# Drains between VectorE's scans and products, and the last batch's chain inside the last group of tiles, in a graph and expert layer

## The reference, cut to what matters

```
h = (xn @ W_gat).reshape(M, 4, 4)
e = leaky_relu(a_src[src] + a_dst[dst])
ee = exp(e - segment_max(e, dst)[dst])
alpha = ee / (segment_sum(ee, dst)[dst] + 1e-16)
agg = segment_sum(h[src] * alpha[:, :, None], dst) + b_gat
scores = layernorm(agg, gamma, beta).reshape(M, 4, 4).mean(1)
w = softmax(top 2 of scores)
out = x + sum over experts e of g_e * (gelu(xn @ W1[e] + b1[e]) @ W2[e] + b2[e])
```

## Time and profile before

| what | value |
|---|---|
| median of 3 runs | 4078.52 us (4076.69 to 4079.31) |
| the profiled execution | 4079.9 us, its span 4078.1 us |
| TensorE matmuls busy | 3314.7 us (81%) |
| GpSimd busy | 2933.2 us (72%) |
| VectorE busy | 2002.3 us (49%) |
| ScalarE busy | 856.3 us (21%) |
| mean granted clock of TensorE | 0.924 of full speed |

### The profile page before, as it was taken

One profiled execution on the slowest core, in us unless ns is written; L12 is line 12 of the kernel. 1 busy time (PEld: TensorE's weight loads), 2 busy tenths in 40 slices (PEclk: granted clock), 3 DMA queues, 4 the chain that ended last, 5 costly groups with the idle time before them and its releaser, 6 DMA issues. The chain is left out here.

```text
span 4078.1 us, 46844 instructions
## 1 busy us (share of the span) xinstructions
PE 3314.7 (81%) x13237; PEld 2233.8 (55%) x13238; DVE 2002.3 (49%) x4747; ACT 856.3 (21%) x2123; POOL 2933.2 (72%) x3018
## 2 busy tenths in 40 slices
PE   0598888998886887878878699999999999994333
PEld 0355555665554655555555366666666666662222
DVE  6577776777765866665454312212223122232555
ACT  6122222222210111111111112222222222220221
POOL 2677777777777777777777777777777777774726
PEclk6799999999998999999999899999999999997665
DMA  8655554554554666667666322222222222224568
GB/s 257 180 136 135 135 135 132 136 133 133 134 140 125 173 173 169 180 174 194 178 175 176 80 79 69 62 63 70 70 70 65 65 71 62 70 73 133 155 183 257
DMA packets 379496, 530.13 MB, mean 130 GB/s; under 512 B 120955, under 2 KB 298459, under 8 KB 379224
## 3 DMA queue, kind: packets, MB, share of 16 engines
q0 software_dynamic: 122976, 244.93, 26.6%
q1 hardware_dynamic: 231599, 261.90, 20.3%
q10 hardware_dynamic: 24776, 21.73, 1.7%
HBM read 381.54 MB, written 146.74 MB: 130 GB/s over the span
## 5 line engine op out<-in xcount | busy, mean ns | idle before, releaser
L824 POOL DMA_INDIRECT rows<-xn_rows,gsrc x1664 | 1613.9, 970 | 509.8 <-issue 509.5
L1414 POOL DMA_INDIRECT nb<-route_rows,idx x1024 | 1011.5, 988 | 318.2 <-issue 303.5
L1130 PE MATMUL PS<-rows,oh 128*128 128x257 f32 x3328 | 867.3, 409 | 276.3 <-DMA rows<-xn_rows,gsrc 275.3
L1130 PEld LDWEIGHTS PS<-rows,oh 128*128 128x128 f32 x3328 | 640.8, 201 | 422.1 <-DMA rows<-xn_rows,gsrc 312.3
L1851 PE MATMUL PS<-arena,hid 128*125 128x256 f32 x3200 | 697.2, 380 | 20.9 <-ACT hid L1763 20.9
L1843 PE MATMUL PS<-x2g,arena 128*128 128x500 f32 x1600 | 676.9, 584 | 17.1 <-DMA x2g<-x_turned 17.1
L1851 PEld LDWEIGHTS PS<-arena,hid 128*125 128x125 f32 x3200 | 598.6, 188 | 129.6 <-issue 33.1
L1731 DVE TENSOR_TENSOR y_sb<-PS,b_b 125x512 f32<-125x512 f32 x200 | 128.7, 685 | 1069.6 <-PE PS L1851 1069.2
L1843 PEld LDWEIGHTS PS<-x2g,arena 128*128 128x128 f32 x1600 | 304.7, 191 | 374.9 <-issue 356.4
L1763 ACT ACTIVATE hid<-PS,b_sb 128x500 f32<-128x500 f32 x400 | 270.8, 677 | 646.5 <-PE PS L1843 646.5
L866 DVE TENSOR_TENSOR oh<-PS,rel 128x1024 f32<-128x1024 f32 x208 | 253.9, 1221 | 9.2 <-issue 1.0
(11 more groups left out here) (341 smaller groups left out, 3524.2 us busy)
## 6 DMA issues: line engine op xcount, KB each, us to landing
y_rows<-y_sb SPq DMA_DIRECT2D x100, 512.0 KB, 2.7
rows<-xn_rows,gsrc POOLq DMA_INDIRECT x1664
arena<-y_rows SPq DMA_DIRECT2D x40, 512.0 KB, 7.0
nb<-route_rows,idx POOLq DMA_INDIRECT x1024
sum_rows<-kept SPq DMA_DIRECT2D x104, 128.5 KB
x_rows<-x SPq DMA_DIRECT2D x100, 128.0 KB, 4.8
m_in<-sum_rows SPq DMA_DIRECT2D x100, 125.5 KB
x_n<-xn_rows SPq DMA_DIRECT2D x100, 125.0 KB
```

Of the source, the lines that this page charges most:

```text
L824: pool.indirect_dma_start(out=rows[w][h][:, q, 0:D], out_offset=None, in_=xn_rows, in_offset=bass.IndirectOffsetOnAxis(ap=gsrc[:, s * HU + ...
L1130: last = mm(SUM[:, 0:D + 1], oh[w][h][:, q, :], rows[w][h][:, q, :], start=h == 0 and q == 0, stop=h == 1 and q == HU - 1)
L1414: pool.indirect_dma_start(out=nb[b % NBUF][:, c, :], out_offset=None, in_=route_rows, in_offset=bass.IndirectOffsetOnAxis(ap=idx[:, b * W ...
```

## The change

It has three parts. (1) VectorE drains before each score scan, before each of the four message products, and between the 20 record scans: 4, 4 and 19 drains a batch. (2) `unit_after` has 5.75(b + 1) + 3.5 rounded down in place of 6(b + 1) + 3: the tiles are 9, 16, 20, 28, 32, 40, 44, 49, 56, 61, 68, 72, 80, 84, 89. (3) Batch 15 isn't late any more. VectorE runs its scores, its records and the lane chain up to `lane_sums` after evicting tile 95, the last of group 23, and the rest after evicting tile 96. ScalarE has its Exp behind the eleventh Gelu of group 24, SP its store behind that of tile 95, and TensorE the two transposes before and after the first tile of group 24's second products.

```diff
 def unit_after(b):
-    t = 6 * (b + 1) + 3
+    t = int(5.75 * (b + 1) + 3.5)
     return t if t % 4 < 2 else t + 4 - t % 4
...
-            batches_after = lambda t: [b for b in range(NB) if unit_after(b) == t]
-            LATE = [b for b in range(NB) if unit_after(b) > NT - 4]
+            batches_after = lambda t: [b for b in range(NB - 1) if unit_after(b) == t]
+            assert unit_after(NB - 2) < NT - 6
...
                     if t % 4 == 0 and t // 4 + 2 < NG:
                         load_group(t // 4 + 2)
+                    if t == NT - 5:
+                        store_records(NB - 1)
...
                 for i in range(YR):
                     final_loads(i)
-                for b in LATE:
-                    store_records(b)
...
                     for h in range(RH):
+                        v.drain()
                         v.tensor_tensor_scan(out=mr[:, h, 1:W + 1], data0=gap[:, at_b], data1=of[:, :, 20 + h],
...
                     for h in range(RH):
+                        v.drain()
                         last = v.tensor_tensor(msg[:, :, 5 * h:5 * h + 5], of[:, :, 5 * h:5 * h + 5], along(dd[:, 0, h, :], 5), ALU.mult)
                     last.then_inc(s_nbf, 1)
                     v.drain()
                     for k in range(20):
+                        if k:
+                            v.drain()
                         last = v.tensor_tensor_scan(out=to[:, :, k], data0=dd[:, 1, k // 5, :], data1=msg[:, :, k],
...
-                for b in LATE:
-                    scores(b)
-                    records(b)
-                for part in (lane_ends, over_lanes, lane_sums, first_maxima, first_records):
-                    part()
+                    if t == NT - 5:
+                        scores(NB - 1)
+                        records(NB - 1)
+                        lane_ends()
+                        over_lanes()
+                        lane_sums()
+                    if t == NT - 4:
+                        first_maxima()
+                        first_records()
...
                         a(hid[:, c, :], HP[c % 4][:, 0:4 * NP], ACT.Gelu, bias=b1_sb[:, c:c + 1]).then_inc(s_hid, 1)
+                        if g == NG - 1 and c == 10:
+                            act.wait_ge(s_dif, NB)
+                            a(dd[:], dd[:], ACT.Exp).then_inc(s_ex, 1)
...
-                for b in LATE:
-                    act.wait_ge(s_dif, b + 1)
-                    a(dd[:], dd[:], ACT.Exp).then_inc(s_ex, 1)
...
-                def group(g, u, pair):
+                def turn_ends():
+                    pe.wait_ge(s_lane, 1)
+                    for k in range(4):
+                        last = nc.tensor.transpose(HP[0][0:20, k * P:(k + 1) * P], ends[:, k, :], ident)
+                    last.then_inc(s_turns, 1)
+
+                def turn_carries():
+                    pe.wait_ge(s_lane, 3)
+                    nc.tensor.transpose(HP[1][:, 0:20], fm[:, 0:P], ident[0:20, 0:20])
+                    nc.tensor.transpose(HP[1][:, 20:40], fx[:, 0:P], ident[0:20, 0:20]).then_inc(s_turns, 1)
+
+                def group(g, u, pair, last_one=False):
...
                     pe.wait_ge(s_hid, g * 16 + 16)
+                    if last_one:
+                        turn_ends()
                     for j in range(4):
...
                         last.then_inc(s_y, 1)
+                        if last_one and j == 0:
+                            turn_carries()
```

More of the change, by code:

```diff
@@ L1860, in _ @@
                 for g in range(NG - 3, NG):
[L1861 to L1868, removed]
+                    group(g, g % 2, g // 2, g == NG - 1)
                 for i, t in enumerate(BY_TURN):
```

## The result

The changed kernel takes 4050.8 us in the median of four executions (4047.4 to 4060.2), against 4078.9 us for the kernel before on the same chip: ratio 0.9933, 95% interval 0.9913 to 0.9952, that is 28 us faster, between 20 and 36. Two later series of the same kernel gave 0.9929 (0.9913 to 0.9946) and 0.9958 (0.9945 to 0.9971). The forecast was 4062 with a range of 4041 to 4086.

The account below looks back on a forecast made before the run. TensorE's expert stage and GpSimd's gathers were taken to bound the kernel together. Stage end +33.5 us and what stood behind it -50 give -16.5, from the 4078.5 us median to 4062, range 4041 to 4086.

Parts of the forecast that it names:

- The two chains end together: TensorE's expert stage and GpSimd's 1024 gathers end together; work moved ahead of one's end must wait for the other.
- The drains free the gathers: Drains between VectorE's scans cut a burst's gather loss from 2.0 to 0.4 us; last gather lands 24 us sooner.
- the Trainium skill's inference: Rival: the scans are not what holds the gathers, so drains give nothing; 4086.5 us, chance 0.08.
- The first rival: Longer drained scan runs hold seven gathers 0.37 us each, 2.6 us a burst; 4094 us, chance 0.12.
- The third: Rival: all gather loss goes, last gather lands at 3677 at the bare pace; 4043 us, chance 0.17.
- The stage's end 52 us behind the last gather's landing: Last group: gathers land at 3695.3, then lane chain, TensorE's restart and second products; last tile evicted at 3747.3.
- Tile 89's wait costs nothing because a longer one follows: VectorE waits some 25 us at tile 89, TensorE stands some 15; free while smaller than the last group's wait.
- First combine 39 us behind the stage's end: After the last eviction: 13 us for own rows to land, weighings of 10 and 15.3 us; first combine at 3786.
- The tail of 276 us is moved as it is.: From first combine to the end the length stays 276 us, so the combine's 16.5 us gain carries to the end.
- The rival for the tail: Tile reads, own rows and stores share transfer engines sooner, losing half the gain; 4070 to 4075 us, chance 0.11.

Follow-up runs that it names:

- without the small sets: Changed kernel with a drain after each fifth record scan and none before score scans and products: 4047.4 us, ratio 0.9911.

## Why the prediction was right, and where its sizes were off

The forecast of 4062 is 11 us above the measured 4050.8, which lies at the edge of the prediction's own narrow range of 4050 to 4073. The direction and the path come from the reasons given; the rest of the 28 us does not.

**The two chains end together.** Right, and the core of it: the drains alone brought nothing, the move alone brought nothing.

**The drains free the gathers.** Right in kind: 20.8 us in the profile, 28 us between the runs with and without them, for 24 predicted; the last gather landed 22.3 us sooner (3699.7 less 2.7, against 3719.3). A burst cost 2.1 us before and 0.6 with 19 drains, for 2.0 and 0.4. By the Trainium skill's inference (SBUF — State Buffer, "Who interferes with whom") two-input instructions don't hold descriptor writing, and the drains would have given nothing (4086.5 us); that taking them out costs 28 us of gathers speaks against it here. Which access of a gather is held, no run shows. The first rival, a hold spread over seven gathers, had the right place and the wrong price: each loses 0.1 us, not 0.37. The third, no loss at all, was not reached with 19 drains; with a drain after each fifth scan it nearly holds for the scans (2.3 us, 0.7 without the small sets), while 14 us and more are lost elsewhere. By the prediction's own figures (1328 against 1278) the bare pace would bring the last gather about 50 us sooner, not 42.

**The stage's end 52 us behind the last gather's landing.** 3751.05 - 3699.70 = 51.4. Right. The small terms differed: TensorE's restart cost 1.9 us rather than 2.3 (8.9 us for the first tile's products in place of 7.0).

**Tile 89's wait costs nothing because a longer one follows.** The wait was 16.0 us, not 25, because tile 88 was already evicted 11 us late (3594.47 less 2.7, against 3580.80 in the earlier trace rows): waits of earlier batches, put at a few us, had held TensorE. It stood 5.9 us at tile 89, for 15 predicted, and was 19 us late in all at the last group. The sum was near, its place wrong. The runs with 6 tiles, where TensorE isn't late, have the same path. The clause "as long as it is smaller than the wait of the last group" proved itself in the run with the chain behind the last tile, where the waits of that spacing bring tile 96's eviction 16 us later (3709.3 against 3693.3 with 6 tiles).

**First combine 39 us behind the stage's end.** 40.5: the own rows' landing was put at 13 us and VectorE started weighing 15.2 us behind the last eviction. The profile names no cause for that idle time; that it waited for the own rows follows from the order of the program, since the gathers at node ends had begun 31 us earlier.

**"The tail of 276 us is moved as it is."** This step failed. It is 266.8 us. The rival for the tail had the sign wrong: I looked for a loss from sharing the transfer engines. Between the starts of the fourth and the fifth weighing (the kernel before first, then the changed one) lie 46.9 and 37.4 us:

```profile
3858.66 0.23 DVE L1616 TENSOR_TENSOR zf<-nb 125x80 f32<-125x80 f32 x1
...
3905.53 0.24 DVE L1616 TENSOR_TENSOR zf<-nb 125x80 f32<-125x80 f32 x1
```

```profile
3848.82 0.23 DVE L1620 TENSOR_TENSOR zf<-nb 125x80 f32<-125x80 f32 x1
...
3886.17 0.23 DVE L1620 TENSOR_TENSOR zf<-nb 125x80 f32<-125x80 f32 x1
```

The drains alone take 47.5, the chain behind the last tile at 5.75 tiles 46.5; the second profile of the changed kernel has 39.3, and without drains it is 39.7. The kernel before and these first two have the gathers at node ends only 41 to 44 us ahead of the first combine, and their tails last 275 to 276 us; the others have them 56 us ahead. In the first three the last of these gathers starts 83 to 86 us behind the first combine, in the others 69 to 71. The run with the last batch at tile 96 and 6 tiles between batches fits less well: it has the lead and the last gather of the first three (44 and 83 us), yet 43.7 us between those weighings and a tail of 271.9. That the shorter overlap of these gathers with the reads and stores of tiles is the cause is argued from these rows; no run changed the overlap alone.

In sum: the path was predicted 16.5 us shorter and is 12 to 15 us shorter in the changed kernel's three profiles. In the first it is 13.5 us shorter, of which the later start takes back 2.7; the tail was predicted unchanged and is 8.8 us shorter. The median's 28 us are 8 more than this execution's, which was the slowest of four. So about half of the 28 us is the path that was predicted; the rest is the tail, which was not, and what the unprofiled executions have beyond it, whose cause stays open.

## What to carry to other kernels

Where two engines' chains end together, speeding up one and moving work ahead of the other's end are each worth nothing; cost them together, and find which wait the moved work would meet. Where GpSimd issues the gathers that a stage waits for, look for gathers longer than their median beside runs of VectorE instructions without a drain, and break such runs seldom: one or three drains in twenty scans served better than nineteen. And weigh such changes by a path between two rows of the profile as well as by medians: here medians of one kernel differed by 17 us between series (4050.8 to 4067.7), the path by 3, if only in one profiled execution of each.

## What the runs showed of the hardware that I had not expected

A run of twenty overlapping scans holds only its last gather. In batches 1 to 14 of the kernel before, gathers that began up to 2.3 us behind the run's start lost 0.06 us or less; the one at 2.78 us lost 2.4, the one at 3.56 lost 1.6. Both end 6.1 us behind the run's start, 0.8 us behind its end. Beginning early is no protection, though. The run of batch 0, whose scans start from a constant, lasts 4.11 us, and the gather that begins 1.05 us into it is held for 3.86 us, again until 0.8 us behind the end:

```profile
2487.06 4.11 DVE L1504 TENSOR_TENSOR_SCAN rec<-dd,msg 128x64 f32<-128x64 f32 x20
...
2488.11 3.86 POOL L1414 DMA_INDIRECT nb<-route_rows,idx  x1 [0.30 <-issue]
```

What decides which gathers get through, no run shows. A run broken once, after 2.8 us, delays no gather by more than 0.06 us in 12 of batches 1 to 14. And drains between all scans are not free for the gathers: nearly each one beside them takes 1.05 us instead of 0.94.
